# Causal attention of 16 heads: two heads of a pair woven by row-tile width, V products per 256 queries, one written order for each engine

## The reference

```python
# x: (2, 1024, 128); W_K, W_Q, W_V: (16, 64, 128); W_O: (128, 1024)
K = einsum('bpd,ihd->biph', x, W_K)      # the same for Q and V
scores = einsum('biph,biqh->biqp', K, Q)
scores = where(tril, scores, -1e10)      # causal
attn = softmax(scores / sqrt(64))
z = einsum('biph,biqp->biqh', V, attn)
out = einsum('bqf,df->bqd', z.reshape(b, q, 16 * 64), W_O)
```

## Time and profile before

| what | us |
|---|---|
| median of three executions | 803.75 |
| all three | 808.1, 803.19, 803.75 |
| the profiled execution | 807.68 |
| its span, first to last instruction | 805.9 |
| PE busy in the span | 699.0 (87%) |
| DVE, ACT, POOL busy | 644.3 (80%), 561.1 (70%), 509.6 (63%) |
| mean granted TensorE clock | 0.972 of 2.4 GHz |

### The profile page before, as it was taken

The page is one execution under the profiler, slowest core; times in us unless marked ns, Lnnn a source line. Parts: engine busy times, 40 slices in busy tenths (PEclk is TensorE's granted clock), DMA queues, the critical chain, the costliest instruction groups (busy, mean ns, idle before and its releaser), DMA issues.

```text
span 805.9 us, 15635 instructions
## 1 busy us (share of the span) xinstructions
PE 699.0 (87%) x4241; PEld 564.2 (70%) x4241; DVE 644.3 (80%) x1373; ACT 561.1 (70%) x1311; POOL 509.6 (63%) x517
## 2 busy tenths in 40 slices
PE   4519999888889898989898989898999999988884
PEld 3418999766667776777677777676777777766763
DVE  7875776687868887878888888888888888887772
ACT  4714555477767777778787778787787777777671
POOL 6853444199887565656565656565656665678993
PEclk9959999999999999999999999999999999999997
DMA  7418222134252425243443425161607061626011
GB/s 225 127 36 189 60 60 56 42 79 110 65 127 53 109 54 115 59 101 72 94 86 73 99 67 120 40 131 35 147 12 160 14 148 24 135 49 132 27 27 29
DMA packets 35478, 68.27 MB, mean 85 GB/s; under 512 B 5264, under 2 KB 26096, under 8 KB 31344
## 3 DMA queue, kind: packets, MB, share of 16 engines
q1 hardware_dynamic: 33136, 63.08, 34.4%
q0 software_dynamic: 2304, 4.72, 2.5%
HBM read 12.73 MB, written 4.72 MB: 22 GB/s over the span
## 4 chain that ended last, share of the span: by engine, by line
PE 34%; POOL 25%; issue 20%; DVE 7%; ACT 6%; DMA 5%; SPq 2%; POOLq 1%; ACTq 0%; DVEq 0%
POOL probs L564 16%; PE ps_big L1201 5%; DMA k_st<-k_parts 5%; PE ps_mid L1214 4%; PE ps_z L1231 4%; PE ps_z L1230 4%; POOL k_parts L508 3%; POOL z_lo L569 3%; ACT probs L724 3%; PE ps_big L1147 2%; DVE pT_lo L997 2%; PE ps_z L1168 2%; PE ps_z L1169 2%; PE ps_big L1148 2%; PE ps_big L1149 2%
## 5 line engine op out<-in xcount | busy, mean ns | idle before, releaser
L564 POOL TENSOR_TENSOR probs<-probs,rden 128x128 f32<-128x128 f32 (+7 forms) x256 | 298.8, 1167 | 187.7 <-DVE rden L984 186.3
L997 DVE TENSOR_TENSOR pT_lo<-ps_mid,pT_hi 128x512 fp32r<-128x512 f32 (+3 forms) x384 | 201.0, 551 | 42.3 <-ACT pT_hi L739 40.2
L739 ACT ACTIVATE pT_hi<-ps_mid 128x512 fp32r<-128x512 f32 (+3 forms) x384 | 174.6, 491 | 71.2 <-PE ps_mid L1214 69.3
L1201 PE MATMUL ps_big<-k_st,q_st 128*128 128x512 f32 (+2 forms) x768 | 218.5, 386 | 0.0
L1214 PE MATMUL ps_mid<-ident,probs 128*128 128x128 f32 x1152 | 177.0, 279 | 36.8 <-DVE pT_lo L997 25.3
L724 ACT ACTIVATE probs<-ps_big,neg_max 128x128 f32<-128x128 f32 (+7 forms) x256 | 190.2, 743 | 15.0 <-DVE neg_max L979 14.0
L979 DVE TENSOR_REDUCE neg_max<-ps_big 128x1 f32<-128x128 f32 (+7 forms) x256 | 191.2, 747 | 1.6 <-PE ps_big L1201 1.0
L1214 PEld LDWEIGHTS ps_mid<-ident,probs 128*128 128x128 f32 x1152 | 133.6, 141 | 80.6 <-DVE pT_lo L997 40.0
L1230 PE MATMUL ps_z<-pT_hi,v_st 128*128 128x512 f32 (+2 forms) x384 | 132.3, 352 | 0.0
L1231 PE MATMUL ps_z<-pT_lo,v_st 128*128 128x512 f32 (+2 forms) x384 | 129.1, 350 | 0.0
L1201 PEld LDWEIGHTS ps_big<-k_st,q_st 128*128 128x128 f32 x768 | 118.3, 194 | 1.0
(11 more groups left out here) (193 smaller groups left out, 1130.1 us busy)
## 6 DMA issues: line engine op xcount, KB each, us to landing
k_st<-k_parts SPq DMA_DIRECT2D x64, 512.0 KB
q_st<-q_parts SPq DMA_DIRECT2D x64, 256.0 KB
y_dram<-y_sb SPq DMA_DIRECT2D x40, 64.0 KB
raw_gu<-in_L_ffn_Wg_dram SPq DMA_DIRECT2D x9, 176.0 KB, 2.3
raw_gu<-in_L_ffn_Wu_dram SPq DMA_DIRECT2D x9, 176.0 KB, 2.6
raw_d<-in_L_ffn_Wd_dram SPq DMA_DIRECT2D x9, 128.0 KB, 2.6
res<-in_L_attn_x_dram SPq DMA_DIRECT2D x4, 256.0 KB, 3.7
xn_dram<-xn SPq DMA_DIRECT2D x4, 256.0 KB, 2.7
```

What stands on the lines that cost most here:

```text
L564: pool.tensor_tensor(rows, rows, col.to_broadcast([P, width]), ALU.mult).then_inc(normed, 1)
L739: nc.scalar.activation(pT_hi[j][buf][:, g * TPB:g * TPB + tiles, (i % TPB) * P:(i % TPB + 1) * P], ps_mid[:, bank, 0:tiles * P].rearrange( ...
L997: nc.vector.tensor_tensor(pT_lo[j][buf][:, kt, q], ps_mid[:, bank, 0:tiles * P].rearrange("p (t q) -> p t q", t=tiles), pT_hi[j][buf][:, k ...
L1201: ins = nc.tensor.matmul(ps_big[:, n % 2, c0:c1], w, k_st[half][h][:, part, c0 - off:c1 - off], start=part == 0 and not masked, stop=part ...
```

## The change

1. The units of a half alternate between the heads: head 0 from wide to narrow, head 1 from narrow to wide (`UNITS`). Even units and the odd ones beside them have 9 key tiles together; odd units are never wider than 512 columns.
2. V products are made per 256 queries (`JOBS`, two units each, `2m + 2` key tiles, always 256 wide; on the last key tile the left 128 columns are a tile of zeros). `pT_hi` and `pT_lo` become one array each with two areas. The products go to two places, `ps_z` and the free second half of odd score bank (`z_bank`).
3. In place of the slots, each engine gets a written order of a half (`PE_ORDER`, `ACT_ORDER`, `DVE_ORDER`, `POOL_ORDER`). Letters: S scores, T transposes (unit.group), V V products (job.piece), M a fill of `ps_misc`, X maximum, E exponentials, R reciprocal, N norm, H and L the copies to `pT_hi` and `pT_lo`, Z and Y the sums of z, C the copies out of `ps_misc`, K POOL's part of k. A "-" means the half before, a "+" the next half. The scores of unit n + 4 now stand before the transposes of unit n, and the exponentials of unit n + 4 right behind the copies of unit n.
4. The order of the projections becomes `MISC_ORDER`: q1 is now the last q block and k0 the last k block, and q1 comes after k0. `stack` waits for these. It still asks for q first.
5. The amount of work per half on DVE, ACT and POOL, the DMAs and their sizes, and the number of score and transpose matmuls stay.

```diff
-        PT_BUFS = [1, 1]
-        pT_hi = [[sb(f"pT_hi{j}{c}", [P, TPB * (j + 1), BLK], F32R) for c in range(PT_BUFS[j])] for j in range(QB)]
...
+        AREA = 2 * (QT + 2)
+        pT_hi = sb("pT_hi", [P, 1 + 2 * AREA, P], F32R)
+        pT_lo = sb("pT_lo", [P, 1 + 2 * AREA, P], F32R)
...
+        z_bank = [ps_z[:, :], ps_big[:, 1, BLK:2 * BLK]]
...
-        AHEAD = 3
-        ORDER = [0, 1, 2, 3, 4, 5, 7, 6]
...
+        UNITS = [(0, 7), (1, 0), (0, 6), (1, 1), (0, 5), (1, 2), (0, 4), (1, 3),
+                 (1, 4), (0, 3), (1, 5), (0, 2), (1, 6), (0, 1), (1, 7), (0, 0)]
+        JOBS = [(0, 3), (1, 0), (0, 2), (1, 1), (1, 2), (0, 1), (1, 3), (0, 0)]
+        ZS = [(0, 1), (1, 0), (1, 1), (0, 0)]
...
-        PROJ_SLOT = {"wqkv": 1, "q0": 2, "q1": 3, "k0": 4, "k1": 6, "v0": 7, "v1": 9, "t0": 11, "t1": 12, "wo": 14}
...
+        PIECES = {8: [(0, 3), (3, 6), (6, 8)], 6: [(0, 3), (3, 6)], 4: [(0, 2), (2, 4)], 2: [(0, 2)]}
...
+        PE_ORDER = read("""
+            Mwqkv T15.0- S4 T0.0 T0.1 Mk1 V6.0- S5 T1.0 Mq0 S6 T2.0 T2.1 V6.1- S7 V6.2- Mk0 T3.0 V7.0- S8 T4.0
+            T4.1 Mv1 S9 V0.0 T5.0 S10 Mq1 T6.0 S11 V0.1 T6.1 V0.2 Mt1 T7.0 S12 V1.0 T8.0 V2.0 T8.1 Mo1- V2.1
+            T9.0 S13 Mv0 S14 T10.0 T10.1 V3.0 Mo0- V3.1 T11.0 T12.0 S15 S0+ T12.1 S1+ T13.0 Mt0 V4.0 T14.0 T14.1
+            S2+ S3+ Mwo V4.1 V5.0 V5.1""")
+        ACT_ORDER = read("""
+            H15.0- Cwqkv E3 H0.0 H0.1 Ck1 E4 H1.0 Cq0 E5 H2.0 H2.1 E6 Z2- Ck0 H3.0 E7 Z3- H4.0 H4.1 E8 Cv1 H5.0
+            E9 Cq1 H6.0 Y1- E10 H6.1 H7.0 Ct1 Y0- H8.0 E11 H8.1 E12 H9.0 Z0 E13 Cv0 H10.0 H10.1 E14 H11.0 H12.0
+            E15 Z1 H12.1 H13.0 E0+ Ct0 E1+ H14.0 H14.1 Cwo E2+""")
+        DVE_ORDER = read("""
+            L14.1- X3 L15.0- Cwqkv R2 X4 R3 L0.0 Ck1 L0.1 X5 L1.0 Cq0 X6 L2.0 R4 X7 L2.1 Z2- L3.0 Ck0 R5 X8 L4.0
+            R6 L4.1 X9 R7 R8 L5.0 X10 R9 Cq1 L6.0 X11 Z3- L6.1 R10 L7.0 Ct1 X12 L8.0 Co1- R11 R12 L8.1 X13 L9.0
+            Z0 X14 L10.0 L10.1 R13 Co0- R14 L11.0 X15 L12.0 X0+ L12.1 L13.0 Z1 X1+ R15 R0+ Ct0 X2+ Cwo R1+ L14.0""")
+        POOL_ORDER = read("""
+            N1 N2 N3 K1 N4 N5 N6 K0 N7 N8 Z1- N9 N10 Z0- N11 N12 N13 N14 N15 N0+""")
+
+        MISC_ORDER = ["wqkv", "k1", "q0", "k0", "v1", "q1", "t1", "o1", "v0", "o0", "t0", "wo"]
...
+        def last_of(kind, p):
+
+            return [n for n in (PROJ_FIRST if isinstance(p, int) and p < 0 else MISC_ORDER) if n[0] == kind][-1]
...
             def stack(p, b):
 
-                k_q1, k_k1 = (1, 3) if b == 1 else (11, 13)
-                before = p if b == 1 else p - 1
-
-                wait(sp, *part_done(before, k_q1))
+                before, made = (p, 0) if b == 1 else (p - 1, 1)
+                wait(sp, *part_done(before, made, last_of("q", before)))
...
-                wait(sp, *part_done(before, k_k1))
+                wait(sp, *part_done(before, made, last_of("k", before)))
...
-            def probs_v(p, b, h, j, k0, k1):
...
+            def probs_v(p, b, job, k0, k1):
...
+                tiles = 2 * m + 2
+                dst = z_bank[job % 2][:, (m % 2) * 2 * P:(m % 2 + 1) * 2 * P]
                 for kt in range(k0, k1):
...
+                    t = pT_tile(job, kt, 0)
+                    at = slice(t, t + 2) if kt < tiles - 1 else slice(0, t + 2, t + 1)
                     w = v_st[b][:, kt, h, :, :].rearrange("p a c -> p (a c)")
...
+                    nc.tensor.matmul(dst, w, pT_hi[:, at, :], start=kt == 0, stop=False, skip_group_check=True)
+                    ins = nc.tensor.matmul(dst, w, pT_lo[:, at, :], start=False, stop=kt == tiles - 1, skip_group_check=True)
```

More of the change, by code:

```diff
@@ L299, in bank_read @@
[L299 to L322, removed]
@@ L347, in group_count, with job_of, last_unit, pT_tile @@
         def group_count(p, n):
-            head, u = divmod(n, QT)
-            return 4 * GPH * p + head * GPH + sum(GROUPS[:u + 1])
+            half, u = divmod(n, UPH)
+            return 2 * GPH * p + half * GPH + sum(GROUPS[:u + 1])
         def group_bank(n, g):
[L353 to L358, removed]
+            return (sum(GROUPS[:n % UPH]) + g) % 2
+        def job_of(n):
+            return 2 * (n % UPH // 4) + n % 2
+        def last_unit(job):
+            return max(u for u in range(UPH) if job_of(u) == job)
+        def pT_tile(job, kt, odd):
+            before = 2 * (2 * JOBS[job - 1][1] + 2) if job % 2 else 0
+            return 1 + AREA * (job // 2 % 2) + before + 2 * kt + odd
         def score_cols(i):
@@ L520, in _ @@
             pool.wait_ge(down_done, SUBS)
[L522 to L525, removed]
+            pool.memset(pT_hi[:, 0, :].bitcast(F32), 0.0)
+            pool.memset(pT_lo[:, 0, :].bitcast(F32), 0.0).then_inc(pads_zero, 1)
             def fetch_y(c, t):
@@ L544, in add_y, with gather_y @@
                 pool.tensor_tensor(res[:, t, :], res[:, t, :], yg[k % 4][:], ALU.add).then_inc(res_done, 1)
[L546 to L550, removed]
+            def gather_y(p, s):
+                c = 0 if p == 0 else 1
                 if s % 2 == 0:
@@ L579, in _, with split_part @@
[L579 to L592, removed]
+            def split_part(p, b, name):
+                pool.wait_ge(part_rounded, pooled_count(p, b, name))
+                raw, hi, lo = part_views(name)
+                pool.tensor_tensor(lo, raw, hi.bitcast(F32), ALU.subtract).then_inc(pool_split, 1)
@@ L593, in _ @@
+            iteration(-1)
+            iteration(0)
             with pool.Fori(1, PAIRS - 1) as p:
[L594 to L597, removed]
+                iteration(p)
+            iteration(PAIRS - 1)
+            iteration(PAIRS)
         @block.scalar
@@ L619, in round_down, with copy_proj @@
                 nc.scalar.activation(down_of(e, 0, slice(0, ILAST), last), raw_d[j][0:ILAST, last, :], ACT.Copy).then_inc(whi_done, 1)
[L621 to L625, removed]
+            def copy_proj(p, b, name, bank=ps_misc[:, :]):
+                b_next = 1 - b
+                act.wait_ge(proj_filled, proj_count(p, b, name))
+                if name[0] == "q" and not (isinstance(p, int) and p < 0):
+                    act.wait_ge(stacked, 16 * STACKS * (2 * p + b + 1))
                 if name == "wqkv":
@@ L743, in move_z, with copy_probs @@
-            def move_z(p, b, h, j):
-                act.wait_ge(z_ready, z_count(p, b, h, j))
+            def copy_probs(p, n, g):
+                i, job = UNITS[n % UPH][1], job_of(n)
+                if n % 4 == 0 and g == 0:
+                    wait(act, pv_done, pv_count(p, n // UPH, job - 3))
+                count = group_count(p, n) - i // TPB + g
+                tiles = min(TPB, i + 1 - g * TPB)
+                bank = group_bank(n, g)
+                act.wait_ge(t_ready, count)
+                t = pT_tile(job, g * TPB, i % 2)
+                nc.scalar.activation(pT_hi[:, t:t + 2 * tiles - 1:2, :],
+                                     ps_mid[:, bank, 0:tiles * P].rearrange("p (t q) -> p t q", t=tiles),
+                                     ACT.Copy).then_inc(pT_copied, 1)
@@ L783, in _, with iteration @@
-            iteration(0, True, False)
+            def iteration(p):
+                for kind, arg, at, b, live in steps(ACT_ORDER, p):
+                    if not live:
+                        continue
+                    if kind == "E":
+                        exp(at, b * UPH + int(arg))
+                    if kind == "H":
+                        k, g = arg.split(".")
+                        copy_probs(at, b * UPH + int(k), int(g))
+                    if kind == "Z":
+                        move_z(at, b, int(arg))
+                    if kind == "Y":
+                        copy_z(at, b, int(arg))
+                    if kind == "C":
+                        copy_proj(at, b, arg)
@@ L1061, in _ @@
+            iteration(-1)
+            iteration(0)
+            with dve.Fori(1, PAIRS - 1) as p:
+                iteration(p)
+            iteration(PAIRS - 1)
+            iteration(PAIRS)
+            for j in BLOCKS:
+                add_x(1, j)
         @block.tensor
@@ L1217, in probs_v, with turn_probs @@
-            def probs_v(p, b, h, j, k0, k1):
-                if k0 == 0:
-                    pe.wait_ge(pT_split, group_count(p, b * UPH + h * QT + last_unit(j)))
-                    wait(pe, z_summed, z_count(p, b, h, j) - 1)
-                if k0 == 0 and h == 0 and j == BLOCKS[0]:
-                    k = 17 if b == 0 else 7
-                    pe.wait_ge(*part_done(p if b else p - 1, k))
-                tiles = TPB * (j + 1)
-                buf = (2 * b + h) % PT_BUFS[j]
+            def turn_probs(p, n, g):
+                i = UNITS[n % UPH][1]
+                if g == 0:
+                    pe.wait_ge(normed, unit_count(p, n))
+                count = group_count(p, n) - i // TPB + g
+                bank = group_bank(n, g)
+                wait(pe, pT_split, count - 2)
+                for c in range(min(TPB, i + 1 - g * TPB)):
+                    kt = g * TPB + c
```

(24 more changed lines are left out.)

357 lines of the change are left out of this document (163 added, 194 removed).

## The result

The changed kernel takes 858.3 us (median of four, 855.6 to 860.0), the kernel before 804.4 us (four, 803.2 to 808.1): 1.066 times as long, 95% interval 1.061 to 1.070. The forecast was slower, 832 us, range 811 to 850. The direction and the place were right, the size was too small, and the time lies outside the range.

What follows compares the result with a forecast made beforehand. No engine was full; PE had 33.9 us of work per 39.1 us half. A late stack and slowed clock made a half 41.3: twelve times 2.2 plus 2, +28.4 on 803.75, gave 832 us, range 811 to 850.

Steps and rivals of the forecast that it cites:

- The stack in the new order: q and k DMAs sent together after q1, 16.3 us: S0+ late by some 5 us, a half 40.5 us against 39.1.
- Walk and floor of the half: One half: 20.7 us of PE work from S0+ to Mq1, 0.9 waits, 2.6 and 16.3 for the stack: 40.5 us.
- Rival 3: Inner halves: q and k transfers fit in 11.5 us and the weave wins, half 36.0, 767 us; chance 0.07.
- V products: Attention on PE: 256-wide products cost 0.3 us more per head, 0.6 per half; weight loads no bound.
- The clock: PE's gap of about 4.5 us in each half slows its clock; 0.8 us per half passed on, bounds 0 and 1.7.
- Edges: Outside the twelve inner halves: first half +2, gathering halves 0 (-3 to +4), prologue and tail 0.
- Rival 2: After S0+: the restart is worse than walked, half 43, 852 us; chance 0.09.
- Rival 1: At the stack wait: stack late but the clock holds, half 40.5, 822 us; chance 0.27.
- Rival 4: No difference: no waits in the first part (39.6 per half) and gathering halves gain 3, 809 us; chance 0.07.

Runs made afterwards that it cites:

- warm: The changed kernel with 19 unused matmuls of 512 columns on PE just before the wait of S0+; 835.4 us, ratio 1.039 to the kernel before.
- dates: The changed kernel with k sent before q and the fills before q1 exchanged, so both k and both q blocks come early; 765.2 us, ratio 0.953.
- old_v256: The kernel before with each 512-wide V matmul cut in two of 256, output off, only time used; 806.5 us, ratio 1.0016.
- dates_q_first: The kernel dates with q's wait and DMAs put in front of k's again; 810.1 us, ratio 1.0045 to the kernel before.
- old_late: The kernel before with q's DMAs sent together with k's, after k1; 895.0 us, ratio 1.114.
- k_first: The changed kernel with SP waiting for k and sending its DMAs before q's; 837.1 us, ratio 1.042 to the kernel before.

## Why the prediction was wrong in size

**Right.** *The stack in the new order.* The forecast said that all eight DMAs go together after q1, that they need 16.3 us and that S0+ is late by some 4.5 us. In the trace they go together, S0+ comes 16.5 us after the first one in the half shown (436.06 to 452.57), and waits 4.73 us. PE's work between the fill of q1 and S0+ was put at 13.8 us. It starts at 433.82 and reaches S0+ at 447.8: 14.0.
*Walk and floor of the half.* Without the fall of the clock the half was to be 40.5 us; warm shows 40.17.
*Rival 3, the weave without the wait,* was priced at 36.0 us per half and 767 us. dates, which gives it its condition, has 35.47 and 765. The time was near, but in part by luck: of the 36.0, 1.5 were to be waits and 34.5 PE's work. In dates PE has no waits in the inner halves, and its work alone takes 35.4 us per half (70.8 per iteration, 70.58 of them busy), so the count of PE's work was 0.9 too low. The low chance was right, as the condition wasn't in the change: dates meets it by the dates, with the same transfers.
*V products.* That their greater number costs nothing by itself is shown (old_v256). The 0.6 us per half for their columns wasn't measured alone.

**Wrong: the step "The clock".** It put the fall at 0.8 us per half, between 0 and 1.7. It cost 2.06 in the inner halves, outside its own bounds. The step took one slow stretch of 3.4 us, partly hidden in the gap. In the trace the slow stretch is 6.8 us in 8 of the 12 inner gaps and 3.4 in the others. At nine of the twelve nearly 80% of it or more lies behind the wait (451.9 to 458.7, with S0+ at 452.57); at the other three 2.6 to 2.8 us of 6.8 fall into the gap. On average 4.6 us at 1.2 GHz lie behind S0+, not 2.4. It also supposed that S0's chain over DVE and ACT hides part of it. Yet PE has no wait at all behind S0+: every matmul between 452.57 and 476.69, where q1 is filled, follows its predecessor, so each us at half speed costs 0.5 us in full. Half of 4.6 is 2.3, near the 2.06 that warm shows. Against the forecast of 41.3 us for a half, the clock adds 1.26 and the rest of the half takes 0.33 less: 42.23. There is a fall around every one of the 15 waits. The Trainium skill ("TensorE: Matmul & The Clock Gate", "HAM oscillation — how this bites in real kernels") says that a DMA wait inside each turn of a loop throttles PE anew each turn; the trace agrees.

**Wrong: the step "Edges".** The first half was put at +2 and is +8.4. Starting with the widest unit wasn't priced: two waits of 2.32 and 1.65 us and 10.2 us of half clock, and then the wait for the stack as in all others. dates has no such wait on the stack and is still at 38.6 there, so some 4 of the 8.4 belong to the start. The last half and tail, put at 0, are +4.1. The last S0+ has its wait and its slow clock as well, and 61.0 us went to 65.1. But the slow clock behind it doesn't explain them: in warm the clock holds there, falls at 807.5 us instead, for 10.2 us, and the stretch still takes 64.3. In dates, which has neither the wait nor a fall behind S0+, it takes 62.8.

In the span the forecast was +28.4 and the measurement +50.6: the inner halves are missing 11.5 us, the first half 6.4, the other edges together 4.3. Another 4 us come from the median: the execution profiled before lay 3.9 us over its median, and that of the changed kernel at its own.

**Wrong reasons that were excluded.** Rival 2 (a bad restart) had the time nearest to the result, 852 us, but not its mechanism: it asked for over 3 us of waits behind S0+, and there are none. Rival 1 (the clock holds) falls with the 15 slow stretches; warm made its condition and has nearly its half. Rival 4 (no waits in the first part, 809 us) falls with 65.7 us of waits on the stack.

**What stays open.** What makes the tail's +4.1 isn't settled: filling the last wait gave back 0.8 (warm), and the order of the last units wasn't tried alone. Whether the transfers could run faster in another form wasn't tried either: the stack runs at 202 GB/s with its engines busy for 0.92 of the time, and each of its eight DMAs reads and writes only 64 of the 128 partitions. The Trainium skill ("DMA: Bandwidth & Descriptors", "Where 436 GB/s comes from") has 435 GB/s as the bound of transfers inside SBUF. The trace's 202 differs from it, and the measurement decides.

## What to carry to other kernels

When an order is rewritten, every date that it keeps implicitly has to be moved too: here a chain of fill, split and 15.6 us of serial DMA needs its place counted back from the first use, and one queue that asks for the later of two inputs first can cost more (45 us, dates against dates_q_first) than the new order wins. Read that from the queue's own rows (issue, engines' share, first use); the engines' busy shares over the span don't show it. Here a wait that emptied TensorE cost its own length and, since TensorE had no wait behind it, also about half of the slow stretch that followed (2.06 us of 4.6). Filler work of just the wait's length gave the second part back, and moving the date gave back both.

## What the runs showed of the hardware

- Added work made a kernel faster: 19 matmuls of 512 columns in the place of each wait (4.5 us) took 858.3 us to 835.4, as the clock stayed at 1.00 from 169 to 807 us.
- How often the clock fell behind the same kind of wait: at 15 of 15 where PE waited 5.0 us on average (old_late) or 4.4 (the changed kernel), at 12 of 15 with 3.4 us (k_first), at 7 of 15 with 2.3 us (dates_q_first).
- Two matmuls of 256 columns with a weight load each cost about as much as one of 512: 0.236 us against 0.23 from start to start, and 384 matmuls more changed the time by less than the measurement tells (1.0016, 0.998 to 1.005, old_v256).
